# Attention values: one matmul of 512 query columns a step in place of two of 256

## The chip, the cores and the metric

The kernel runs on one NeuronCore of one Trainium2 chip. The metric is the device time of one execution in microseconds (us); three runs of the kernel before gave 1795.75, 1789.95 and 1794.83 us, median 1794.83 us.

TensorE is the matrix engine. The trace splits it into PE (matmuls) and PEld (weight loads). DVE is VectorE, ACT is ScalarE, POOL is GpSimd, SP issues the DMAs. Each engine works through its own instructions in program order; they meet at semaphores.

## The reference, cut to what matters

Input is one sequence of 2048 tokens with 128 features, in fp32. Two layers follow each other, each with attention over 16 heads of 8 features and a feed-forward part (layer 0: a ternary gated network; layer 1: eight experts, top two).

```python
# layer 0 (causal)                                # layer 1 (latent, not causal)
q, k, v = split(x @ w_qkv.T)                      query, key, value from latents, rotated
q, k = rope(q), rope(k)
scores = einsum('bhsd,bhtd->bhst', q, k) / scale  attn = einsum('bhqd,bhkd->bhqk', query, key) / scale
scores = where(causal, scores, -inf)
attn = softmax(scores, axis=-1)                   attn = softmax(attn, axis=-1)
out = einsum('bhst,bhtd->bhsd', attn, v)          out = einsum('bhqk,bhkd->bhqd', attn, value)
x = x + out.reshape(B, S, D) @ w_out.T            x = x + out.reshape(b, s, d) @ Wo_w + Wo_b
```

## The kernel before, in words

The program runs norm, projection, attention, output, norm and feed-forward for each layer, one after the other. The change is in `attention_phase` (L307), which both layers call.

**Units, steps, half steps.** The 2048 queries are cut into four chunks of 512 columns, the 16 heads into four groups of four. A unit is one chunk with one group, so each layer has 16 units, worked one after the other. A unit walks over key tiles of 128 keys; one key tile with all four heads is a step. Layer 1 has 16 steps in each unit. Layer 0 is causal: the units of chunk c (0 to 3) have 4c+1 full steps, then a step "mixed" from parts of two key tiles of the diagonal, and a "narrow" step. A step has two halves with two heads each (the narrow step of layer 0 has one half).

**What TensorE is given in a half step** (`unit`, L509): two score matmuls (`scores`, L463, keys x queries, 64 rows each, 512 columns, L478), then the maxima planned for this half (`score_maxima`, L440, L452), then a part of the values of the step before (`values_part`, L502). In half 1 of step 0 there are also four matmuls that build the queries of the unit after next (L427, L429), and three halves (layer 1) or two (layer 0) before the end four that turn the softmax shift of the next unit (L437). The order is written out by hand; `plan` (L377) only spreads the maxima of the next two units over the halves. That is one maxima item a half in most of layer 1, none in its last unit, 12 in all in the one before it, and between one and one and a half in layer 0, where its later units have few or none as well.

**Scores and their three banks.** A score matmul writes one of three PSUM banks (`E_BANKS = 3`, L24), taken in turn. ACT reads each bank with an exponential (L593) into one of eight tiles `probs`. `wait_bank` (L417) holds the matmul number e until ACT has finished with bank user e-3:

```python
def wait_bank(e):
    if e >= E_BANKS:
        pe.wait_ge(e_done, e - E_BANKS + 1)
```

With four scores in a step, called s0, s1 (half 0) and s2, s3 (half 1) below, s2 waits for the exponential of the previous step's s3, and s3 waits for the exponential of s0 of its own step.

**Maxima.** For the softmax shift, TensorE computes all scores once more, two heads (1024 columns) at a time, into one of two pairs of PSUM banks, and DVE takes the maximum (L612). An item waits until DVE is done with the item two before it.

**Values.** `values` (L483) multiplies V by the exponentials of the previous step: four heads, each on 128 rows and 9 output columns in its own 32-column strip of the array, into the accumulator bank 7. Each fp32 matmul is shown as two MATMUL records and two weight loads. In most steps half 0 multiplies query columns 0 to 255 and half 1 columns 256 to 511. Three cases already go "whole", all columns at once in half 1: the values of step 0 of each unit (issued in step 1), those of the narrow step, and those issued in a step with one half. ACT reuses a `probs` tile once `pv_done` says that the values of two steps before are done (L591). In diagonal steps of layer 0 POOL masks the exponentials (L556) before the values use them. At the end of a unit DVE copies the accumulator out (L643).

Of the kernel before, what the change touches and what calls it, by code (L numbers as in the profile page):

```python
# [19 lines left out]
HD = D // H  # L20
T = S // P
CW = 512
C = S // CW
TC = CW // P  # L24
HG = 4
# [281 lines left out]
def attention_phase(nc, k, layer):  # L307

    causal = layer == 0
# [12 lines left out]
    def score_steps(n):  # L322
        c = units[n][0]
        whole = lambda kt: [[[(j, kt, 0, 0)] for j in (2 * b, 2 * b + 1)] for b in (0, 1)]
        if not causal:
            return [whole(kt) for kt in range(T)]
        first, second, third, fourth = range(TC * c, TC * c + TC)
        mixed = [[[(j, second, P, 0), (j, fourth, 3 * P, 3 * P)] for j in (2 * b, 2 * b + 1)] for b in (0, 1)]
        narrow = [[[(half, third, 2 * P, 0), (2 + half, third, 2 * P, 2 * P)] for half in (0, 1)]]
        return [whole(kt) for kt in range(first + 1)] + [mixed, narrow]  # L330

    def diagonal_steps(n):
        return range(len(score_steps(n)) - 3, len(score_steps(n))) if causal else range(0)

    step_list = [score_steps(n) for n in range(NU)]
# [6 lines left out]
    def pieces(n, s):  # L342
        for b, half in enumerate(step_list[n][s]):
            for x, job in enumerate(half):
                for j, kt, low, at in job:
                    yield j, kt, low, at, prob_tile(n, s, b, x)
# [22 lines left out]
    def masks_done(n, s):  # L369
        count = 0  # L370
        for m in range(n + 1):
            for t in diagonal_steps(m):
                if (m, t) <= (n, s):
                    count += sum(1 if [at for _, _, _, at in half[0]] == [0, 2 * P] else len(half[0]) for half in step_list[m][t])
        return count
# [23 lines left out]
    with ExitStack() as ctx:  # L399
        sem = lambda s: ctx.enter_context(nc.semaphore(f"{name}_{s}"))  # L400
        e_ready, e_done, pv_done, acc_free = sem("e_ready"), sem("e_done"), sem("pv_done"), sem("acc_free")
# [5 lines left out]
        acc = k.bank[7]  # L407
# [8 lines left out]
        def _(pe):  # L416
# [63 lines left out]
                        if piece == len(jobs[x]) - 1:  # L480
                            mm.then_inc(e_ready, 1)

            def values(n, s, part):  # L483
                g = units[n][1]
                last = part == "second" or part == "whole"
                if s in diagonal_steps(n):
                    pe.wait_ge(masked, masks_done(n, s))
                else:
                    pe.wait_ge(e_done, e_number["scores", n, s, 1, 1] + 1)
                if s == 0:  # L490
                    pe.wait_ge(acc_free, n + 1)
                todo = sorted(pieces(n, s), key=lambda item: (item[1], item[0]))
                for j, kt, low, at, tile in todo:
                    middle = (CW - low) // 2
                    a, z = {"whole": (0, 2 * middle), "first": (0, middle), "second": (middle, 2 * middle)}[part]
                    end = s == len(step_list[n]) - 1 and last and kt == todo[-1][1]
                    mm = pe.matmul(acc[32 * j:32 * j + HD + 1, low + a:low + z], k.V9[:, kt, g * HG + j, :],  # L497
                                   k.probs[:, tile, at + a:at + z], start=(s == 0), stop=end)
                if last:
                    mm.then_inc(pv_done, 1)  # L500

            def values_part(n, s, b, of):  # L502
                if s == 0 or s == len(step_list[n]) - 1 and causal or of == 1:
                    if b == of - 1:
                        values(n, s, "whole")
                else:
                    values(n, s, ("first", "second")[b])

            def unit(n):  # L509
                slots = plan(n)  # L510
                for h, (s, b) in enumerate(halves[n]):
                    scores(n, s, b)
                    if h == 1 and n + 2 < NU:
                        build_queries(n + 2)
                    if h == shift_at[n] and n + 1 < NU:
                        turn_shift(n + 1)
                    for m, i in slots[h]:
                        score_maxima(m, i, 1 + EXTRA_PASSES[units[n][0]] if causal else 1)
                    of = len(step_list[n][s])
                    if s:  # L520
                        values_part(n, s - 1, b, of)
                    elif n:
                        values_part(n - 1, len(step_list[n - 1]) - 1, b, of)
# [8 lines left out]
            for b in (0, 1):  # L532
                values_part(NU - 1, len(step_list[NU - 1]) - 1, b, 2)
# [670 lines left out]
```

## Time and profile before

| | value |
|---|---|
| median of three runs | 1794.83 us (1789.95 to 1795.75) |
| profiled execution, span from first to last instruction | 1802.3 us |
| PE busy | 1667.7 us, 93% |
| DVE busy | 1157.5 us, 64% |
| ACT busy | 1115.9 us, 62% |
| mean granted TensorE clock | 0.927 |

Of the profiled execution the profile gives the span alone, and no time of its own beside it. Busy time counts the union of an engine's instructions; matmuls overlap and their ends are modelled, so a busy PE isn't a PE at its peak. The units of layer 0 fill about 69 to 511 us of the span, those of layer 1 about 829 to 1508 us.

### The profile page before, as it was taken

The numbers are of one execution on the slowest core, as the hardware profiler recorded it, in microseconds if no ns is written. First come the engines' busy times: TensorE is split into PE (matmuls) and PEld (weight loads), VectorE is DVE, ScalarE is ACT, GpSimd is POOL, SyncE is SP. The second block draws the span as 40 slices with busy tenths as digits, with TensorE's granted clock in tenths as the row PEclk, the third lists the DMA queues.
The fourth block names the chain that finished last, engine by engine and source line by source line (L and its number), as shares of the span: only waits on it lengthen the run. The fifth ranks groups of instructions, "written<-read, shape, count | busy, mean of one in ns | idle before, by whom it ended". The sixth has DMA issues, their size and how long they took to land. (4 is left out here: it accounts for less than half of the span.)

```text
span 1802.3 us, 31760 instructions
## 1 busy us (share of the span) xinstructions
PE 1667.7 (93%) x12488; PEld 768.9 (43%) x12488; DVE 1157.5 (64%) x1566; ACT 1115.9 (62%) x1996; POOL 116.3 (6%) x206
## 2 busy tenths in 40 slices
PE   6889899999989997878999999999999998699999
PEld 3444343343344443323333333333333334477776
DVE  7677989997141112598999999999999834311111
ACT  3547587788852221315888888888888885244343
POOL 3121110100000000200000000000000000000000
PEclk9569999999999997756999999999999999599999
DMA  3100000000000001000000000000000000000000
GB/s 104 65 1 1 1 2 1 1 2 2 1 1 0 0 0 55 0 1 1 1 2 1 1 1 2 1 1 1 1 1 2 1 1 1 24 13 24 12 23 23
DMA packets 16772, 17.13 MB, mean 10 GB/s; under 512 B 2995, under 2 KB 13696, under 8 KB 16128
## 3 DMA queue, kind: packets, MB, share of 16 engines
q1 hardware_dynamic: 16639, 15.32, 2.7%
q8 instruction: 89, 1.46, 0.3%
q14 instruction: 44, 0.35, 0.1%
HBM read 14.26 MB, written 1.05 MB: 8 GB/s over the span
## 5 line engine op out<-in xcount | busy, mean ns | idle before, releaser
L612 DVE TENSOR_REDUCE maxp<-banks 128x2 f32<-128x1024 f32 (+3 forms) x800 | 942.9, 1200 | 137.1 <-PE banks L452 71.1
L593 ACT ACTIVATE probs<-banks 128x512 f32<-128x512 f32 x1568 | 843.1, 596 | 203.9 <-PE banks L478 157.0
L497 PE MATMUL banks<-probs,V 128*9 128x256 f32 (+3 forms) x6016 | 487.3, 398 | 3.7 <-POOL probs L556 3.0
L478 PE MATMUL banks<-Q,K 64*128 64x512 f32 (+3 forms) x1664 | 435.0, 484 | 8.4 <-ACT probs L593 5.0
L452 PE MATMUL banks<-K,Q 64*128 64x512 f32 (+3 forms) x1664 | 375.8, 434 | 35.0 <-DVE maxp L612 34.4
L478 PEld LDWEIGHTS banks<-Q,K 64*128 64x128 f32 x1664 | 180.0, 188 | 363.9 <-ACT probs L593 287.0
L452 PEld LDWEIGHTS banks<-K,Q 64*128 64x128 f32 x1664 | 177.7, 198 | 85.6 <-DVE maxp L612 70.3
L497 PEld LDWEIGHTS banks<-probs,V 128*9 128x9 f32 x6016 | 91.4, 89 | 252.5 <-ACT probs L593 190.8
L1004 DVE SCALAR_TENSOR_TENSOR x<-banks,wts,x 128x128 f32<-128x128 f32 x128 | 36.1, 345 | 196.4 <-PE banks L967 196.4
L992 ACT ACTIVATE work<-banks,eb 128x512 f32<-128x512 f32 x128 | 86.3, 688 | 104.7 <-PE banks L958 102.6
L967 PEld LDWEIGHTS banks<-work 128*128 128x128 f32 x1024 | 118.1, 192 | 11.5 <-issue 11.5
L958 PE MATMUL banks<-xnT,work 128*128 128x512 f32 x256 | 116.3, 603 | 5.3 <-DMA eb<-in_eb 5.3
L967 PE MATMUL banks<-work 128*128 128x128 f32 x1024 | 118.2, 275 | 0.0
L792 PE MATMUL banks<-work,flex 128*128 128x512 f32 x256 | 110.5, 592 | 0.0
L542 POOL CAST Q<-Q 32x512 fp32r<-32x512 f32 x64 | 39.0, 610 | 725.2 <-ACT Q L579 723.2
L830 DVE TENSOR_TENSOR work<-banks,s_rows 128x128 f32<-128x128 f32 x16 | 3.5, 284 | 122.4 <-PE banks L799 122.4
L579 ACT ACTIVATE Q<-banks 32x512 fp32r<-32x512 f32 x64 | 37.7, 589 | 66.2 <-PE banks L437 65.1
L643 DVE COPY outT<-banks 128x512 f32<-128x512 f32 x32 | 21.9, 684 | 87.2 <-PE banks L497 87.2
L792 PEld LDWEIGHTS banks<-work,flex 128*128 128x128 f32 x256 | 48.6, 190 | 61.2 <-issue 61.2
L815 ACT ACTIVATE work<-banks,sh 128x512 f32<-128x512 f32 x32 | 22.0, 687 | 82.7 <-PE banks L792 82.7
L958 PEld LDWEIGHTS banks<-xnT,work 128*128 128x128 f32 x256 | 47.7, 194 | 56.7 <-issue 52.4
L556 POOL TENSOR_SCALAR_AFFINE_SELECT probs<-probs 128x256 f32<-128x256 f32 (+1 forms) x112 | 47.9, 441 | 365.0 <-ACT probs L593 364.3
(127 smaller groups left out, 855.4 us busy)
## 6 DMA issues: line engine op xcount, KB each, us to landing
tables<-in_tables SPq DMA_DIRECT2D x2, 2048.0 KB, 10.3
work<-in_ew SPq DMA_DIRECT2D x16, 256.0 KB, 2.9
flex<-in_h SPq DMA_DIRECT2D x2, 1024.0 KB, 8.4
x<-in_x SPq DMA_DIRECT2D x4, 256.0 KB, 3.9
out<-x SPq DMA_DIRECT2D x4, 256.0 KB, 2.3
cst<-in_consts SPq DMA_DIRECT2D x1, 865.0 KB, 6.0
flex<-in_w SPq DMA_DIRECT2D x3, 256.0 KB, 3.0
flex<-in_w_qk SPq DMA_DIRECT2D x1, 256.0 KB, 6.1
```

The costliest lines, as they stand in the source:

```text
L452: mm = pe.matmul(out, k.Q[rows, n % 3, b, t * P:(t + 1) * P], k.K[rows, 2 * g + b, a * CW:a * CW + w], start=True, stop=True)
L478: mm = pe.matmul(ebank(e)[:, at:at + CW - low], k.K[rows, 2 * g + block, kt * P:(kt + 1) * P], k.Q[rows, n % 3, block, low:CW], start=True ...
L497: mm = pe.matmul(acc[32 * j:32 * j + HD + 1, low + a:low + z], k.V9[:, kt, g * HG + j, :], k.probs[:, tile, at + a:at + z], start=(s == 0) ...
L542: pool.tensor_copy(k.Q[shift_rows(half), n % 3, 1, :], k.Q[shift_rows(half), n % 3, 0, :]).then_inc(spread_done, 1)
L556: pool.affine_select(out=part, in_=part, compare_op=ALU.is_ge, fill=0.0, base=0, pattern=[[0, part.shape[1]], [1, P]], channel_multiplier= ...
L579: copy = act.activation(k.Q[shift_rows(half), n % 3, 0, :], ebank(e)[shift_rows(half), :], ACT.Copy)
L593: act.activation(k.probs[:, number % 8, :], ebank(e), ACT.Exp, scale=scale).then_inc(e_done, 1)
L612: dve.tensor_reduce(dst, src, AX.X, ALU.max).then_inc(m_done, 1)
L792: mm = pe.matmul(hb[m % 2][:, :], w[:, b, m * P:(m + 1) * P], src[:, b, :], start=(b == 0), stop=(b == HB - 1))
L958: pe.matmul(ub[m][:, :], k.ew1[:, q, m * P:(m + 1) * P], k.xnT[:, c * CW:(c + 1) * CW], start=True, stop=True).then_inc(up_ready, 1)
L967: mm = pe.matmul(yb[c % 2][:, t * P:(t + 1) * P], k.hid[:, c % 2, b, t * P:(t + 1) * P], k.ew2[:, q, b, :], start=(b == 0), stop=(b == HB ...
L992: act.activation(k.hid[:, c % 2, m, :], ub[m][:, :], ACT.Gelu, bias=k.eb1[:, q, m:m + 1]).then_inc(act_ready, 1)
```

## The change

`values` loses its argument `part`: it always multiplies columns `low` to 511 of each piece with one call, and always reports `pv_done`. `values_part` calls it in the last half of a step alone. The arithmetic is the same.

```diff
-            def values(n, s, part):
+            def values(n, s):
                 g = units[n][1]
-                last = part == "second" or part == "whole"
                 if s in diagonal_steps(n):
                     pe.wait_ge(masked, masks_done(n, s))
                 else:
@@
                 for j, kt, low, at, tile in todo:
-                    middle = (CW - low) // 2
-                    a, z = {"whole": (0, 2 * middle), "first": (0, middle), "second": (middle, 2 * middle)}[part]
-                    end = s == len(step_list[n]) - 1 and last and kt == todo[-1][1]
-                    mm = pe.matmul(acc[32 * j:32 * j + HD + 1, low + a:low + z], k.V9[:, kt, g * HG + j, :],
-                                   k.probs[:, tile, at + a:at + z], start=(s == 0), stop=end)
-                if last:
-                    mm.then_inc(pv_done, 1)
+                    end = s == len(step_list[n]) - 1 and kt == todo[-1][1]
+                    mm = pe.matmul(acc[32 * j:32 * j + HD + 1, low:CW], k.V9[:, kt, g * HG + j, :],
+                                   k.probs[:, tile, at:at + CW - low], start=(s == 0), stop=end)
+                mm.then_inc(pv_done, 1)
 
             def values_part(n, s, b, of):
-                if s == 0 or s == len(step_list[n]) - 1 and causal or of == 1:
-                    if b == of - 1:
-                        values(n, s, "whole")
-                else:
-                    values(n, s, ("first", "second")[b])
+                if b == of - 1:
+                    values(n, s)
```

## Rows read from the trace of the kernel before

**Rows 1.** The page's costliest groups: busy us and mean ns; idle before, its releaser.

```profile
L612 DVE TENSOR_REDUCE maxp<-banks 128x2 f32<-128x1024 f32 (+3 forms) x800 | 942.9, 1200 | 137.1 <-PE banks L452 71.1
L593 ACT ACTIVATE probs<-banks 128x512 f32<-128x512 f32 x1568 | 843.1, 596 | 203.9 <-PE banks L478 157.0
```

**Rows 2.** Windows, 13 units of layer 1: us, busy of each engine, clock, DMA.

```profile
880.00:1429.00 549.00, 545.36 (x4986) 196.58 (x4986) 513.07 (x468) 475.86 (x882) 15.89 (x26) 1.00 0.01 1
```

**Rows 3.** Timeline, a common step of layer 1: start, length, engine, idle before.

```profile
1133.77 8.48 DVE L612 TENSOR_REDUCE maxp<-banks 128x2 f32<-128x1024 f32 x7
...
1137.80 0.50 PE L478 MATMUL banks<-Q,K 64*128 64x512 f32 x2
...
1138.13 0.40 PE L452 MATMUL banks<-K,Q 64*128 64x512 f32 x2
...
1138.46 0.62 PE L497 MATMUL banks<-probs,V 128*9 128x256 f32 x8
...
1140.25 0.50 PE L478 MATMUL banks<-Q,K 64*128 64x512 f32 x2
```

**Rows 4.** Timeline, step 1 of a unit of layer 1, where values go whole.

```profile
1132.46 0.50 PE L478 MATMUL banks<-Q,K 64*128 64x512 f32 x2
...
1132.80 0.40 PE L452 MATMUL banks<-K,Q 64*128 64x512 f32 x2
...
1133.04 0.39 PE L478 MATMUL banks<-Q,K 64*128 64x512 f32 x1
1133.06 2.07 ACT L593 ACTIVATE probs<-banks 128x512 f32<-128x512 f32 x4 [0.81 <-PE banks L478]
...
1133.71 0.50 PE L478 MATMUL banks<-Q,K 64*128 64x512 f32 x1 [0.28 <-ACT probs L593]
...
1133.71 0.73 PE L452 MATMUL banks<-K,Q 64*128 64x512 f32 x2
...
1134.37 1.05 PE L497 MATMUL banks<-probs,V 128*9 128x512 f32 x8
...
1135.35 0.50 PE L478 MATMUL banks<-Q,K 64*128 64x512 f32 x2
```

**Rows 5.** Groups by line and form: the value matmuls of 256 and 512 columns.

```profile
L497 PE MATMUL banks<-probs,V 128*9 128x256 f32 x5504 | 428.8, 384 | 2.5 <-POOL probs L556 1.8 <-ACT probs L593 0.7
L497 PE MATMUL banks<-probs,V 128*9 128x512 f32 x256 | 39.2, 690 | 0.0
```

**Rows 6.** Timeline, last unit of layer 1 (no maxima): step 1, then common steps.

```profile
1471.64 1.75 PE L478 MATMUL banks<-Q,K 64*128 64x512 f32 x4
...
1473.32 1.05 PE L497 MATMUL banks<-probs,V 128*9 128x512 f32 x8
...
1474.29 0.50 PE L478 MATMUL banks<-Q,K 64*128 64x512 f32 x2
...
1484.39 0.50 PE L478 MATMUL banks<-Q,K 64*128 64x512 f32 x2
...
1486.68 0.50 PE L478 MATMUL banks<-Q,K 64*128 64x512 f32 x2
```

**Rows 7.** Timeline, the unit of layer 1: its last two steps' first scores.

```profile
1164.76 0.50 PE L478 MATMUL banks<-Q,K 64*128 64x512 f32 x2
...
1170.75 0.50 PE L478 MATMUL banks<-Q,K 64*128 64x512 f32 x2
```

**Rows 8.** Timeline, layer 0, chunk 2, more than one maxima item a half.

```profile
308.29 6.87 DVE L612 TENSOR_REDUCE maxp<-banks 128x2 f32<-128x1024 f32 x6
...
312.95 0.49 PE L452 MATMUL banks<-K,Q 64*128 64x512 f32 x2 [0.36 <-DVE maxp L612]
```

**Rows 9.** Windows, the start of the last unit of layer 1: columns as in 2.

```profile
1463.60:1470.50 6.90, 6.75 (x42) 2.29 (x42) 0.01 (x1) 3.83 (x7) 1.22 (x2) 0.51 0.01 2
```

**Rows 10.** Timeline of that window: two half steps.

```profile
1465.74 0.79 PE L478 MATMUL banks<-Q,K 64*128 64x512 f32 x2
...
1467.44 0.79 PE L478 MATMUL banks<-Q,K 64*128 64x512 f32 x2
```

## The prediction

> **What bounds the kernel now.** I read the page's groups first. The reader sees there that the two great consumers beside TensorE, the maxima on DVE (943 us) and the exponentials on ACT (843 us), both have idle time whose releaser is a matmul [rows 1]. The windows place this: over 13 units of layer 1 PE is busy 545 of 549 us, DVE 513 (93%), ACT 476 (87%), at full clock [rows 2]. So PE's stream looks like the bound, with two engines close behind. That is an average; the timeline of one step says what orders it. A common step, from its first scores to the next step's, takes 1140.25 - 1137.80 = 2.45 us [rows 3]: in each half 0.33 us from scores to maxima, 0.33 us from maxima to values, and 0.55 us for the four values of 256 columns before the next scores. DVE does seven maxima in 8.48 us beside it [rows 3], 1.21 us each, one a half, so it only just keeps up.
>
> Two halves of 0.55 us look like waste beside one whole. But the same trace shows what the uncut form does, because step 1 of every unit already has it. There the step goes from 1132.46 to 1135.35, 2.89 us (2.88 before rounding) [rows 4]. The same form repeats in the 14 units of layer 1 that have two maxima a step and run at full clock, at 2.87 to 2.88 us each.
>
> **Where the 0.43 us come from.** In rows 4 the first scores start at 1132.46, maxima at 1132.80, and with no values between, s2 already starts at 1133.04. Its partner s3 starts only at 1133.71, and its row names the releaser: 0.28 us idle, until an ACT exponential [rows 4]. That is the three-bank wait: s3 may not write until the exponential of s0, of its own step, is done. ACT's first exponential starts at 1133.06, 0.60 us after s0, and takes 0.60 [rows 1, 4]; 0.05 us later s3 goes, 1.25 us after the step began. This time is a latency, not work: scores (0.5), handover (0.1), exponential (0.6), handover. In the old form the first 0.55 us of values lie inside it. In the new form nothing is left to put there. Queued behind the waiting s3 on PE are this half's maxima, then all values, then the next step: 1133.71 to 1134.37 until the values start, and 0.98 us until the next scores (1135.35). Sum: 1.25 + 0.66 + 0.98 = 2.89 us against 2.45.
>
> **The change, term by term.** *Removed on PE.* The 256-column form has 5504 records [rows 5], 128 of which are whole values of the narrow steps; the other 5376 are 336 values of a step at 16 records, 8 of which go each time. Two halves cost 2 x 0.55 = 1.10 us and the whole one 0.98, so PE gives up 0.12 us a step. This is in the 2.88.
> *Added wait.* As above; net +0.43 us for a full step with one maxima item a half. It's self-consistent: ACT's four exponentials end 1133.06 + 2.07 = 1135.13, ahead of the next scores at 1135.35, so each step starts as rows 4 did. DVE needs 2.4 us of the 2.88 and can't be late. The accumulator is written by the same engine in order; the values end at 1134.37 + 1.05 = 1135.42, and the exponential that reuses their tiles can start 0.60 us after the next scores, at 1135.95. No DMA or SP instruction moves.
>
> *Layer 1.* Units 0 to 13, steps 2 to 13: 14 x 12 = 168 steps x 0.43 = 72.7 us. The last two steps take 1170.75 - 1164.76 = 5.99 us now [rows 7]; the turn of the shift sits behind s3 in the first of them, and I add the parts (1.73 until the exponential of s1 frees its bank, 0.59 turn, 0.44 maxima, 0.98 values, then 2.88) to 6.62, +0.6 us x 14 = 8.8. Step 0 has the query builds, which wait for ACT already; I take +0.2 (bounds 0 and 0.43), x 13 = 2.7, and 0.8 for the same steps of the last two units. The last unit has no maxima: its steps are 1486.68 - 1484.39 = 2.28 us now (2.29 by the printed starts), and its step 1 in whole form 1474.29 - 1471.64 = 2.65 [rows 6], +0.37 x 14 = 5.2. The one before it has a maxima item in 12 of 32 halves; between both cases, +0.30 x 13 = 3.9. Layer 1: 94 us.
>
> *Layer 0.* Full steps paced like layer 1 are 3, 7 and 11 in each of two units of chunks 1, 2, 3: 42 x 0.43 = 18.2. In the other two units of chunks 1 and 2 (20 steps) DVE is the pace: six maxima in 6.87 us without a gap, and PE waits for DVE [rows 8]. A step with three items lasts 3.4 us there, and 2.89 plus one more pair of matmuls (0.33) fits inside, so the wait is covered; if the cover is gone it costs the full 0.43. I take 0.15 (bounds 0 and 0.43): 3. The last two units have few or no maxima: 22 x 0.30 = 6.6. Twelve mixed steps gain back part, since values that now wait for POOL's masks come later anyway: 0.12 each, 1.4. Chunk 0 has no step that changes. Layer 0: 29 us.
>
> Sum +123 us on a span of 1802.3: 1925. The profile gives that span alone, 7.5 us above the median of the runs; on the median it's 1794.8 + 123 = 1918 us. Bounds by the terms: with those that have zero as a bound at zero, the mixed steps too, and the 35 steps of few or no maxima at 0.1 in place of 0.3, +109; with all of these at 0.43, +138. So 1904 to 1933.
>
> **Rivals.** *A, faster.* PE is 99% busy [rows 2], and the change takes 0.12 us of PE work out of each step. If PE's stream alone were the bound, 336 x 0.12 = 41 us go and the time is 1754. For it: PE's share, and DVE's seven maxima without a gap. Against it: rows 4, where the less work takes longer; it decides only if s3 is not held by the exponential, and the row names that releaser.
> The Trainium skill (TensorEngine Tiling, Key Properties) says that "changing tiling mode (not just tile) drains the TensorE"; scores use 64-row tiles and values 32-column strips, so the change saves one such switch in and out a step. By that rule alone the result is rival A. The trace agrees that a switch has a price, within the 0.12 us of rows 3 and 4, and shows the larger wait beside it.
>
> *B, no change.* DVE is 93% busy [rows 2]. Were it the pace in all stretches as in rows 8, PE's wait would lie under it and the time would stay at 1795. Against it: in whole-form steps DVE has to wait as well, since 2.88 us is above its 2.4.
>
> *C, slower still: the clock falls.* Where PE stood idle before the last unit the granted clock is 0.51 for 6.9 us, that is mostly the lower of the two levels, 1.2 GHz [rows 9], and a half step there takes 1467.44 - 1465.74 = 1.70 us [rows 10] against 1.14 (half of 2.28, rows 6), +0.56. In the last units without maxima the new steps leave PE idle for longer than any long stretch at full clock now. If about 25 such steps run at the lower level, that is 25 x 2 x 0.56 = 28 us, and the time is 1946. Stretches with maxima have a whole-form step once a unit at clock 1.00 [rows 2], so I don't expect it there.
> The Trainium skill (TensorE: Matmul & The Clock Gate, Part 1) has the throttled clock as the default that activity releases; by it C gets its chance, and rows 9 agree.
>
> *D, it isn't what it says.* Columns `low` to 511 are the same set as both halves, so no work disappears but the doubled instructions.
>
> **Chances.** The forecast 0.82, C 0.10, A 0.05, B 0.03. Less than 0.3% (5.4 us) can't be told from no change here. Faster is A, 0.05; same is B, 0.03; slower 0.92. The range has the bounds of the terms, some 8 us below for cover I don't see, and reaches up to C: 1895 to 1948 us.
>
> **What would show it.** In the changed profile: L497 with 3328 records in place of 6016 if none are missing, those of 256 columns 128 alone; common steps of layer 1 at 2.88 us with s3 1.25 us after s0, and its idle time put down to the exponential L593; no gap left for PE in front of values; last unit 2.65 us a step; DVE's idle in layer 1 up by 0.4 us a step, with a matmul L452 as releaser; layer 0's chunk 2 almost unmoved where DVE paces. Wrong would be: common steps at or under 2.45 us (A or B), or steps at another length with a clock under 1.00 (C). The forecast also fails if s3's wait shrinks because something else moves up.

## The result, and the profile after

The changed kernel takes 1947.66 us (median of four runs, 1943.16 to 1956.19) against 1795.16 us before: 1.086 times as long, 95% interval 1.083 to 1.089. That is 152 us more, where +123 were forecast. The interval puts it at 1944 to 1955 us, with the forecast's upper end of 1948 inside; taken against the median that the forecast started from, that end is a ratio of 1.085, a shade under the measured 1.086.

The profiled execution has a span of 1954.5 us at a mean clock of 0.912 (before 1802.3 and 0.927); it is the slowest of the four, the others had a clock of 0.917 to 0.921. L497 has become L494 and has 3328 records, as forecast. First the common step of layer 1, in the timeline (start, length, engine, idle before it); it answers to [rows 3] and looks like [rows 4]:

```profile
1146.01 0.50 PE L478 MATMUL banks<-Q,K 64*128 64x512 f32 x2
...
1146.34 0.40 PE L452 MATMUL banks<-K,Q 64*128 64x512 f32 x2
...
1146.58 0.39 PE L478 MATMUL banks<-Q,K 64*128 64x512 f32 x1
1146.60 2.06 ACT L586 ACTIVATE probs<-banks 128x512 f32<-128x512 f32 x4 [0.81 <-PE banks L478]
...
1147.25 0.50 PE L478 MATMUL banks<-Q,K 64*128 64x512 f32 x1 [0.28 <-ACT probs L586]
...
1147.91 1.04 PE L494 MATMUL banks<-probs,V 128*9 128x512 f32 x8
...
1148.89 0.50 PE L478 MATMUL banks<-Q,K 64*128 64x512 f32 x2
```

From 1146.01 to 1148.89 are 2.88 us. s3 starts 1.24 us after s0, with the exponential as releaser. ACT, which had short gaps, now idles 0.81 us a step, for matmuls that come late.

The waits (in total, times, longest) and the groups of the page say the same over the whole run:

```profile
PE banks L478 <- ACT probs L586: 100.0, 336, 0.5
```

```profile
L605 DVE TENSOR_REDUCE maxp<-banks 128x2 f32<-128x1024 f32 (+3 forms) x800 | 949.9, 1201 | 240.6 <-PE banks L452 170.0
L586 ACT ACTIVATE probs<-banks 128x512 f32<-128x512 f32 x1568 | 815.1, 601 | 386.2 <-PE banks L478 384.1
```

The wait is counted 336 times, as many as there are changed values, though not in quite the same steps (step 1 of each unit had it before). Against [rows 1], DVE's wait for L452 went from 71 to 170 us, and ACT's idle time from 204 to 386. PE's work alone doesn't set the step: s3 waits for ACT, and ACT's next exponential for s3. DVE waits behind these two.

To place the time, the turns of the shift (L437) in the last unit of layer 0, the first of layer 1 and the last of layer 1, before:

```profile
470.56 0.66 PE L437 MATMUL banks<-identr,shiftM 128*128 128x128 f32 x4
...
826.44 1.11 PE L437 MATMUL banks<-identr,shiftM 128*128 128x128 f32 x4
...
1463.75 0.66 PE L437 MATMUL banks<-identr,shiftM 128*128 128x128 f32 x2 [1.69 <-DVE shiftM L639]
```

and after:

```profile
495.71 0.55 PE L437 MATMUL banks<-identr,shiftM 128*128 128x128 f32 x3
...
870.04 0.69 PE L437 MATMUL banks<-identr,shiftM 128*128 128x128 f32 x2
...
1598.62 0.66 PE L437 MATMUL banks<-identr,shiftM 128*128 128x128 f32 x2 [2.27 <-DVE shiftM L632]
```

Up to the last unit of layer 0 the kernel has lost 25.2 us, from there to layer 1 18.4, over the 15 units of layer 1 that follow 91.3, and in the last unit and behind it the rest of 152.2, 17.3. The forecast had 25.9, 3.3, 88.9 and 5.2. The two long stretches are right; the two last units are not. The windows (us, busy of PE, PEld, DVE, ACT, POOL, granted clock, DMA) show their slow part, and in the last row a part of layer 1's last unit at full clock:

```profile
502.60:557.20 54.60, 50.64 (x185) 12.65 (x184) 0.00 (x0) 27.76 (x53) 2.98 (x7) 0.50 0.00 0
1598.30:1639.30 41.00, 37.80 (x123) 9.75 (x123) 0.86 (x2) 20.58 (x39) 1.22 (x2) 0.50 0.00 0
1641.00:1656.00 15.00, 11.93 (x68) 3.46 (x64) 0.00 (x0) 11.55 (x24) 0.00 (x0) 1.00 0.00 1
```

Layer 0's last unit ran at 0.50, the 1.2 GHz level, from its second step to its end; layer 1's for its first 41 of 62 us. A step there, in the timeline of the same kernel:

```profile
1605.55 1.22 PE L478 MATMUL banks<-Q,K 64*128 64x512 f32 x3
1607.09 0.79 PE L478 MATMUL banks<-Q,K 64*128 64x512 f32 x1 [0.32 <-ACT probs L586]
1607.81 1.89 PE L494 MATMUL banks<-probs,V 128*9 128x512 f32 x8
1609.63 0.79 PE L478 MATMUL banks<-Q,K 64*128 64x512 f32 x2
```

1609.63 - 1605.55 = 4.08 us, against 2.64 at full clock in the same unit. Eleven such steps in layer 0 and nine in layer 1 make 20 x 1.44 = 29 us. With the parts of steps at both ends it is more: from the turn of their shift to their last values the two units take 60.9 and 61.6 us, and 42.4 and 47.1 in a kernel below (`e5_maxima_in_half0`) that has the same steps there at full clock, 33 us less. The forecast's 3.3 and 5.2 us on top of the 40.9 and 43.6 of before come to 3.6 us more than these 89.4 (42.4 + 47.1 before rounding), as the kernel before had a low stretch of its own in each. What is left is 29 us, the difference to the forecast.

Where the clock fell differs. In layer 1 it fell in the gap of 2.27 us ahead of the unit. In layer 0 there is no such gap: it fell 6.9 us behind the turn of the shift, in step 1, with pauses of 0.22 and 0.25 us before it, and in the kernel before at the same place, 6.6 us behind its turn. Here after, then before:

```profile
502.19 0.50 PE L478 MATMUL banks<-Q,K 64*128 64x512 f32 x1 [0.25 <-ACT probs L586]
502.61 1.90 PE L494 MATMUL banks<-probs,V 128*9 128x512 f32 x8
```

```profile
477.13 0.79 PE L478 MATMUL banks<-Q,K 64*128 64x512 f32 x1 [0.26 <-ACT probs L593]
```

Up to there both kernels give TensorE the same instructions in the unit. So the new form is not needed for this fall; what differs is how long the clock stays down, 6.8 us before and 54.6 after.

### The profile page after: what moved, and what is told of

Its sections match the earlier page's. It is cut to its first block and busy times, and to the rows that moved or that the text cites. A ratio compares the mean times of both kernels' runs of the same rounds, so it can differ in the third digit from the quotient of the medians.

```text
span 1954.5 us, 26384 instructions
## 1 busy us (share of the span) xinstructions
PE 1729.7 (88%) x9800; PEld 773.4 (40%) x9800; DVE 1167.3 (60%) x1566; ACT 1087.5 (56%) x1996; POOL 116.5 (6%) x206
## 5 line engine op out<-in xcount | busy, mean ns | idle before, releaser
L586 ACT ACTIVATE probs<-banks 128x512 f32<-128x512 f32 x1568 | 815.1, 601 | 386.2 <-PE banks L478 384.1
L478 PE MATMUL banks<-Q,K 64*128 64x512 f32 (+3 forms) x1664 | 551.1, 478 | 104.3 <-ACT probs L586 100.0
L478 PEld LDWEIGHTS banks<-Q,K 64*128 64x128 f32 x1664 | 227.7, 195 | 633.2 <-ACT probs L586 527.4
L452 PE MATMUL banks<-K,Q 64*128 64x512 f32 (+3 forms) x1664 | 446.1, 451 | 31.7 <-DVE maxp L605 30.7
L494 PE MATMUL banks<-probs,V 128*9 128x512 f32 (+3 forms) x3328 | 441.8, 608 | 0.1
L452 PEld LDWEIGHTS banks<-K,Q 64*128 64x128 f32 x1664 | 195.5, 199 | 82.3 <-DVE maxp L605 67.2
L494 PEld LDWEIGHTS banks<-probs,V 128*9 128x9 f32 x3328 | 51.5, 89 | 136.2 <-ACT probs L586 107.4
```

The costliest lines, as they stand in the source:

```text
L452: mm = pe.matmul(out, k.Q[rows, n % 3, b, t * P:(t + 1) * P], k.K[rows, 2 * g + b, a * CW:a * CW + w], start=True, stop=True)
L478: mm = pe.matmul(ebank(e)[:, at:at + CW - low], k.K[rows, 2 * g + block, kt * P:(kt + 1) * P], k.Q[rows, n % 3, block, low:CW], start=True ...
L494: mm = pe.matmul(acc[32 * j:32 * j + HD + 1, low:CW], k.V9[:, kt, g * HG + j, :], k.probs[:, tile, at:at + CW - low], start=(s == 0), stop ...
L586: act.activation(k.probs[:, number % 8, :], ebank(e), ACT.Exp, scale=scale).then_inc(e_done, 1)
```

## Experiments

The theory: a three-bank ring makes s3 wait 1.25 us after s0; what stands between them is free, and the whole form leaves too little there. Rivals: the long value matmuls themselves, DVE's banks, or the place of the values. For the 29 us beyond it: what lowers the clock in the last units, and what brings it back. Kernels without an interval had one profile and one time, so differences of a few us between them say nothing.

**Score banks, first set.** Four kernels: split or whole, three or five banks. To free banks, DVE reads little of each maximum (`...` stands for the rest of a line; the branch for two heads is changed alike):

```diff
-        mpair = lambda m: k.banks[:, 3 + 2 * (m % 2):5 + 2 * (m % 2), :]
+        mpair = lambda m: k.banks[:, 5:7, :]
-                if m >= 2:
-                    pe.wait_ge(m_done, m - 1)
+                if m >= 1:
+                    pe.wait_ge(m_done, m)
-                    src, dst = mpair(m)[:, :, 0:w], ...
+                    src, dst = mpair(m)[:, :, 0:64], ...
-E_BANKS = 3
+E_BANKS = 5        # in two of the four
```

> Base of a set of four. Left out: DVE takes each maximum over the first 64 columns of a bank only (so the softmax shift is not the true maximum); the maxima then need one pair of banks, not two. Values are split in halves as in the kernel before, three score banks. Both theories (three-bank wait; TensorE's own stream as the bound): a common step of layer 1 stays near 2.45 us, s3 about 1.22 us after s0; layer 0's stretches paced by DVE go faster, so the whole is 1750 to 1790 us.

> As the base of the set (maxima over 64 columns, one pair of banks, shift not the true maximum), values whole, three score banks. Theory, s3 waits for the exponential of s0 in a three-bank ring: common step of layer 1 at 2.88 us, s3 1.24 us after s0, the whole about 130 to 170 us over the base. Rival, DVE or its bank pairs make the delay: with DVE nearly idle the step falls to about 2.3 us and the whole under the base.

> As the base of the set, values split, but five score banks. Theory: s3 no longer waits for s0's exponential; the step is TensorE's own stream, 2 x (0.34 + 0.33 + 0.55) = 2.43 us, hardly below the base's 2.45, so the whole is within 1% of the base. Rival, the bank ring plays no part: the same.

> As the base of the set, values whole and five score banks. Theory: the wait is gone, s2 and s3 start together 0.24 us after the maxima, and the saving on TensorE shows: 0.34 + 0.24 + 0.34 + 0.33 + 0.98 = 2.2 us a step, 0.2 below split with five banks, about 50 to 70 us less over both layers. Rival, the long value matmuls themselves delay scores or exponentials: the step stays at 2.88 us whatever the banks.

Measured: with three banks 1830.3 us split and 1975.6 whole, +145; with five banks 1796.5 split and 1779.8 whole, -17. With three banks and DVE nearly out of the way the whole step is still 2.87 us, s3 1.23 us after s0. Three expectations missed. The base is 1830 and not under 1790: a unit of layer 1 takes 42.4 us as before, but the last unit of layer 0 turns its shift at 502.6 us in place of 470.6; probably since one pair of maxima banks lets no item run ahead (from 130 to 470 us DVE waits 174 us for L452, where it was 11), with 93 us of lower clock from 85 us up to there, against 38 before. Split with five banks is 1.8% under that base, where 1% was expected. And whole with five banks didn't reach 2.2 us a step but 2.53, against 2.42 split. Its timeline says why:

```profile
1129.88 0.40 PE L478 MATMUL banks<-Q,K 64*128 64x512 f32 x2
1130.42 0.50 PE L452 MATMUL banks<-K,Q 64*128 64x512 f32 x2 [0.15 <-DVE maxp L605]
1130.85 1.05 PE L494 MATMUL banks<-probs,V 128*9 128x512 f32 x8
1131.83 0.50 PE L478 MATMUL banks<-Q,K 64*128 64x512 f32 x2
```

s2 and s3 start together, as expected. But the second maxima item waits for DVE's read of the first in the single pair. The set had put a new wait in place of the old one. So the -17 us is not the gain of a common step: 15 units of layer 1 are 7.5 us slower whole than split, the two last units 8.5 us faster, and up to layer 0's last unit the split kernel had 22 us more of lower clock. This pair shows that the 145 us go with five banks, and no more.

**Score banks, second set.** That wait goes if nothing reads the banks: DVE's maxima read a constant tile, and PE waits for no reader.

```diff
-        mpair = lambda m: k.banks[:, 3 + 2 * (m % 2):5 + 2 * (m % 2), :]
+        mpair = lambda m: k.banks[:, 5:7, :]
-                if m >= 2:
-                    pe.wait_ge(m_done, m - 1)
-                    src, dst = mpair(m)[:, :, 0:w], ...
+                    src, dst = k.ident[:, :].rearrange("p (i w) -> p i w", i=2), ...
-E_BANKS = 3
+E_BANKS = 4        # in two of the three
```

> Base of a second set. Left out: DVE's maxima read a constant tile of 128 x 128 in place of the banks, and TensorE's maxima matmuls wait for no reader (the shift is a constant). So no maxima wait is left, unlike in the first set. Values whole, three score banks. Theory (three-bank wait): common step of layer 1 still 2.88 us, s3 1.24 us after s0.

> As the base of the second set, values split in halves, four score banks. Theory: TensorE's own stream, 2.43 us a step, a shade below the 2.45 of the kernel before.

> As the base of the second set, values whole, four score banks. Theory: with four banks s3 waits for the exponential of the s3 before it, which is long done; nothing else holds the stream, so 0.34 + 0.24 + 0.33 + 0.33 + 0.98 = 2.20 us a step, 0.23 us below split with four banks; over 336 steps 60 to 80 us less than that one. Rival, in the first set whole with five banks was held near 2.4 us by the values or by ACT and not by the single pair of maxima banks: then it stays near 2.4 us here too.

Measured: 1842.0, 1669.8 and 1594.8 us. With four banks whole beats split by 75 us; with three it loses 172 to split with four (split with three was not run in this set). The timelines of the step, whole with three banks:

```profile
1201.05 0.50 PE L476 MATMUL banks<-Q,K 64*128 64x512 f32 x2
...
1202.29 0.49 PE L476 MATMUL banks<-Q,K 64*128 64x512 f32 x1 [0.28 <-ACT probs L584]
...
1203.92 0.50 PE L476 MATMUL banks<-Q,K 64*128 64x512 f32 x2
```

split with four:

```profile
1200.74 0.50 PE L476 MATMUL banks<-Q,K 64*128 64x512 f32 x2
...
1203.16 0.50 PE L476 MATMUL banks<-Q,K 64*128 64x512 f32 x2
```

whole with four:

```profile
1201.15 0.50 PE L476 MATMUL banks<-Q,K 64*128 64x512 f32 x2
1201.48 0.40 PE L450 MATMUL banks<-K,Q 64*128 64x512 f32 x2
1201.72 0.52 PE L476 MATMUL banks<-Q,K 64*128 64x512 f32 x2
1201.95 0.52 PE L450 MATMUL banks<-K,Q 64*128 64x512 f32 x2
1202.40 1.05 PE L492 MATMUL banks<-probs,V 128*9 128x512 f32 x8
1203.38 0.50 PE L476 MATMUL banks<-Q,K 64*128 64x512 f32 x2
...
1204.52 1.05 PE L492 MATMUL banks<-probs,V 128*9 128x512 f32 x8
```

2.87, 2.42 and 2.23 us. The last alternates with 2.12 (values at 1202.40 and 1204.52), 2.17 on average. DVE is out of the first and the wait is unchanged, so DVE's banks are not its cause; the value matmuls are as long in the last and it is gone, so nor are they. Shown, then: the ring of three banks. The saving in TensorE's stream that the change promises is real too, 0.25 us a step, once the fourth bank is there. Here the sign of the change hangs on the banks: the whole units of layer 1 are 3.1 us shorter than the split ones (37.5 against 40.6), at full clock.

**The place of the values.** Whole values in half 0:

```diff
-                if b == of - 1:
+                if b == 0:
                     values(n, s)
```

> Values whole, but in half 0 of the next step in place of half 1. Theory: the three-bank wait is about any score pair with too little in front of it. Now s1 of the next step waits for s2's exponential, since only maxima lie between; the step is again 2.88 us, the whole within 1% of the changed kernel. Rival, the wait hangs on where the values stand against the exponentials that they read (half 1 is late enough, half 0 isn't): the step is longer by 0.1 us or more, 25 us in all.

Measured: 1975.6 us, 1.4% above the changed kernel. The common step is the same 2.88 us:

```profile
1148.76 1.04 PE L494 MATMUL banks<-probs,V 128*9 128x512 f32 x8
1149.74 0.50 PE L478 MATMUL banks<-Q,K 64*128 64x512 f32 x2
...
1150.32 0.39 PE L478 MATMUL banks<-Q,K 64*128 64x512 f32 x1
1150.99 0.49 PE L478 MATMUL banks<-Q,K 64*128 64x512 f32 x1 [0.28 <-ACT probs L586]
...
1151.64 1.05 PE L494 MATMUL banks<-probs,V 128*9 128x512 f32 x8
```

The waiting matmul is now in the other half, as the theory has it. The total missed the 1%, and hides more than it shows. The last unit of layer 0 turns the shift at 527.9 us, 32 later than in the changed kernel, and the 15 units of layer 1 take 17 us more; but both last units ran at full clock and took 30 us less. In layer 0 values in half 0 stand close behind POOL's masks in the diagonal steps, and the clock was low for 89 us between 85 us and there, against 38 in the changed kernel; which of the two costs the 32 us stays open.

**Maxima into the wait.**

```diff
+        for first in range(0, number - 1, 2):
+            slots[first], slots[first + 1] = slots[first] + slots[first + 1], []
         return slots
```

> The changed kernel with the maxima items of both halves in half 0, ahead of s2 and s3. Theory: work moved into the wait is free, s3 stays at 1.24 us after s0, then 0.43 us to the values and 0.98 to the next scores: 2.65 us a step in place of 2.88, about 0.23 us x 250 steps = 55 us less, 1885 to 1900 us, and still above the kernel before. Rival, the two pairs of maxima banks pass the delay on (the second item waits for DVE in half 0): the step stays above 2.8 us.

Measured: 1870.2 us, ratio to before 1.042 (1.036 to 1.048), 15 us under the expectation's lower end. The step:

```profile
1153.08 0.50 PE L480 MATMUL banks<-Q,K 64*128 64x512 f32 x2
1153.41 0.69 PE L454 MATMUL banks<-K,Q 64*128 64x512 f32 x4
1153.95 0.87 PE L480 MATMUL banks<-Q,K 64*128 64x512 f32 x2
1154.75 1.05 PE L496 MATMUL banks<-probs,V 128*9 128x512 f32 x8
```

From the values before, at 1152.10, to these are 2.65 us, as expected. The last units are 33 us shorter than in the changed kernel, while layer 0 up to its last unit is 10 us longer. They are the key to the clock. They have no maxima, so their steps are those of the changed kernel. This one also had the gap ahead of the last unit; and yet the window behind it is at full clock:

```profile
1525.13 0.63 PE L439 MATMUL banks<-identr,shiftM 128*128 128x128 f32 x4 [2.28 <-DVE shiftM L634]
```

```profile
1530.00:1560.00 30.00, 23.83 (x134) 6.73 (x133) 0.69 (x1) 23.61 (x47) 0.00 (x0) 1.00 0.00 1
```

So whole steps without maxima can keep a full clock when they find it. One profile doesn't make a rule; the traces of the other kernels, at the end of this section, bear it out.

**Split in the last units alone.**

```diff
-                if s == 0 or s == len(step_list[n]) - 1 and causal or of == 1:
+                if s == 0 or s == len(step_list[n]) - 1 and causal or of == 1 or n < NU - 1:
```

> Values whole as in the changed kernel, but split in halves as before in the last unit of each layer (no maxima there). Theory, the clock fell in those two units because the whole form leaves TensorE idle: about 29 us of lost clock and 8.5 us of three-bank wait go, so 1908 to 1916 us, with the clock at full in both units but for some 7 us at their start. Rival, the fall comes from the gap before the unit and would last as long anyway: only 8.5 us go, 1939 us, and 40 us or more of lower clock stay.

Measured: 1917.6 us, ratio to before 1.067 (1.061 to 1.072), 30 us under the changed kernel and 2 above the expectation. The low stretch at the start of layer 1's last unit lasted 13.7 us in place of 41, and in layer 0's there was none. The rival's 1939 us is excluded: all four runs lie between 1912 and 1919 us.

**Filler.**

```diff
+                    if n == NU - 1 and b == 0 and s >= 1 and len(step_list[n][s]) == 2:
+                        if s == 1:
+                            pe.wait_ge(m_done, m_base[NU])
+                        for pair in (0, 1):
+                            for half in (0, 1):
+                                rows = slice(HALF * half, HALF * half + HALF)
+                                pe.matmul(mpair(pair)[:, half, :], k.Q[rows, n % 3, 0, 0:P],
+                                          k.K[rows, 2 * units[n][1], 0:CW], start=True, stop=True)
```

> The changed kernel with work added: in the last unit of each layer, half 0 of each step from step 1 on, TensorE multiplies four unused tiles (the form of two maxima items, into the banks that nothing reads any more), where it otherwise waits for s0's exponential. Theory, idle TensorE lowers the clock: the four lie inside the 0.7 us wait, the step stays at 2.65 us at full clock, and the whole falls by 20 to 29 us to 1919 to 1928 us although more is computed. Rival, the clock fell for the gap ahead of the unit: no recovery, 1948 us or more, as the added work costs at the lower clock.

Measured: 1923.3 us, ratio to before 1.070 (1.065 to 1.076): 24 us faster than the changed kernel with 112 matmuls more. The step is no longer, 1605.30 - 1602.66 = 2.64 us from values to values:

```profile
1602.66 1.05 PE L494 MATMUL banks<-probs,V 128*9 128x512 f32 x8
1603.63 0.50 PE L478 MATMUL banks<-Q,K 64*128 64x512 f32 x2
1603.97 0.63 PE L518 MATMUL banks<-K,Q 64*128 64x512 f32 x4
1604.44 0.93 PE L478 MATMUL banks<-Q,K 64*128 64x512 f32 x2
1605.30 0.62 PE L494 MATMUL banks<-probs,V 128*9 128x512 f32 x4
```

In layer 0 the clock did not fall; in layer 1 it fell ahead of the first filler and came back 2 us after it, 10.2 us in all. That the filler brought it back is not shown by that alone, as the next kernel tells.

**Layer 1 alone.** `or of == 1 or not causal` in the condition of the kernel before.

> The kernel before with whole values in layer 1 alone. If the two layers add up: layer 1 has cost about 91 us up to its last unit and 17 in it and after it, layer 0 the other 44, so 1900 to 1910 us. Rival, what layer 0 lost is a clock state that carries over: then under 1890 us or above 1925.

Measured: 1897.6 us, 2 us below the expectation, beside 1789.6 for the kernel before on the same chip: +108. The other 44 of 152 are layer 0's, as the turns had it (25.2 and 20.0 for its last unit). The layers add up to within 10 us, but not better. In the profile layer 1 costs 89.9 us over its 15 units and 8.5 behind them, not 17: its last unit has the very instructions of the changed kernel and the same gap of 2.27 us ahead, but a low clock for 13.7 us alone.

```profile
1550.30:1563.90 13.60, 12.64 (x43) 3.30 (x39) 0.69 (x1) 7.09 (x14) 1.22 (x2) 0.50 0.01 1
```

**The low clock in the last units, over all profiles with three score banks.** How long it lasted, in us (0 is full clock from the turn of the shift to the end), and PE's gap ahead of the turn in layer 1:

| kernel | form in the last units | layer 0 | layer 1 | gap, layer 1 |
|---|---|---|---|---|
| before | split | 6.8 | 6.8 | 1.69 |
| `e3_split_last_units` | split | 0 | 13.7 | 2.27 |
| `e6_split_3banks` | split | 3.4 | 0 | 0.24 |
| `e2_whole_layer1_only` | split, whole | 0 | 13.7 | 2.27 |
| changed kernel | whole | 54.6 | 41.0 | 2.27 |
| `e6_whole_3banks` | whole | 54.6 | 0 | 0.98 |
| `e1_whole_in_half0` | whole | 0 | 0 | 1.28 |
| `e5_maxima_in_half0` | whole | 0 | 0 | 2.28 |
| `e7_free_whole_3banks` | whole | 0 | 0 | 0.45 |
| `e4_filler` | whole, filler | 0 | 10.2 | 2.27 |

In layer 1 the clock fell in five of the six kernels with a gap of 1.69 us or more and in none of the four with 1.28 or less, whatever the form. In these units it never fell among the common whole steps, behind step 1. But the three long stretches all belong to the whole form.

## Why the prediction was right and wrong

- *Step 1 of every unit shows the new form* [rows 4]: right. 2.88 us forecast, 2.88 measured, same wait, same releaser. DVE's idle time for L452 rose by 0.41 us for each of layer 1's 240 changed values, as forecast. One reading was off without harm: DVE's 1.21 us a maximum [rows 3] is the pace of the half step; six in a row take 1.15 each [rows 8].
- *The wait is the three-bank ring*: right, shown by the two sets; 0.12 us less work on PE a step can't be had while s3 waits.
- *Layer 1 up to its last unit*, +88.9: right in size, +91.3. A common unit got 5.9 us longer where the terms give 6.0. Four of them got 7.1 to 7.3, each with a low stretch of the clock of 3.4 us. "I don't expect it there" was wrong, at about 1.2 us each.
- *Layer 0 up to its last unit*, +25.9: right as a sum, +25.2, with some luck. Chunk 0, which has no changed step, came out 4.6 us faster, and the rest cost 29.7. In chunk 2 the first unit that DVE paces moved by 2.2 us and the second by 0.9, each with 7 steps at 0.15 forecast: the cover was partly gone in the first.
- *Query builds and the end of a unit*: right. Step 0 takes 4.29 us against 4.09, and a unit's last two steps 6.60 against 5.99.
- *No-maxima steps*, 2.65 us: right at full clock, 2.64.
- *The clock in the last units*: this is the step that failed. The sum took the last units at full clock, +5.2 and +3.3 us; the low clock stood outside it as rival C at 0.10. In the event C came, at 29 us against the 28 it was priced at, and it moved the time from 1918 to 1948, the edge of the range. The price was right by luck of two errors: 25 steps at +1.12 us were assumed, 20 at +1.44 came. The reason given for C, new steps that leave PE idle and so lower the clock, was only half right as well. Rows 9 show the low clock already in the kernel before, where it was over after 6.8 us; the same happened there in layer 0's last unit. What I missed is that the fall was no risk of the new form but a thing that had happened before, and the question was how long it lasts. What decides that is open: the same instructions gave 41.0 and 13.7 us in layer 1. The turn's row of the kernel before shows a gap of 1.69 us and a fall; with this in view C deserved more than 0.10.
- *Rivals A, B, D*: A's saving exists, and shows only with a fourth bank. B fell: DVE waits 99 us more for maxima. D was the plain statement that no arithmetic goes, and holds.

The Trainium skill (TensorEngine Tiling, Key Properties) says that a change of tiling mode drains TensorE. Whole against split at four banks, 2.17 against 2.42 us a step, agrees with a price for the switch that is saved; but half of the value matmuls go as well, and no run here tells the two apart.

No full kernel that was run beats the kernel before. The way that the second set points to would need four score banks, four for maxima and one accumulator, nine in all; the kernel has eight.

## What to carry to other kernels

When an instruction is cut in two and spread over a loop, ask what its parts stand in front of before joining them: a matmul, its eviction and the reuse of the bank form a latency ring (1.25 us here), and with few banks the pieces between are what fills it. Look for a corner of the loop that already has the new form; its row in the old trace is the best price there is. Count the clock's falls in the old profile too, and ask of each how long it would last in the new form. One profile of each kernel is not enough for that: compare all that you have.

## What the hardware showed

The same whole steps without maxima ran 30 us at full clock with the maxima moved (PE busy 23.83 of 30 us, the window above) and stayed at the lower level in the changed kernel, for 41.0 us in layer 1 (busy 37.80) and 54.6 in layer 0 (busy 50.64). PE looked busier at the lower level, as a matmul record of 512 columns lasts 0.79 us there and 0.50 at full clock, and the clock stayed down. Whether a gap of 2.3 us ahead of the unit brought the fall also differed: 2.27 us did in four kernels, 2.28 us with the maxima moved didn't; 1.69 did, 1.28 and less in four kernels didn't. Once down, the clock was back after 3.4 to 13.7 us under split steps, after 10.2 with filler, and after 13.7, 41.0 and twice 54.6 us under whole ones. Splitting the last units or filling their waits gave 30 and 24 us back, over four runs each. What decides at the gap, and why a low stretch under whole steps ends now early, now late, is open.
